# A two-layer graph network: the turn of z by a crossbar transpose DMA in place of TensorE, and two weight slots in place of three

## The reference

```
h = max(layernorm(x), 0);  x = x + GAT(relu(GAT(h, W1, ...)), W2, ...)    # layers 1 and 2
h = max(layernorm(x), 0);  x = x + GCN(relu(GCN(h, W1, ...)), W2, ...)    # layers 3 and 4
gat_conv: h = x @ W;  alpha = softmax over each node's edges of leaky_relu(a_src[src] + a_dst[dst]);  out = segment_sum(alpha * h[src]) + b
gcn_conv: h = x @ W;  out = segment_sum(h[src] * dinv[src] * dinv[dst]) + b
```

## Time and profile before

| | |
|---|---|
| three runs | 2389.22, 2389.45, 2395.45 us |
| median | 2389.45 us |
| span of the profiled execution | 2395.2 us |
| instructions | 45,199 |
| PE, PEld busy | 95%, 61% |
| DVE, ACT, POOL busy | 67%, 39%, 39% |
| DMA | 482.51 MB, mean 201 GB/s |

### The profile page before, as it was taken

The page is one execution under the profiler, slowest core; times in us unless marked ns, Lnnn a source line. Parts: engine busy times, 40 slices in busy tenths (PEclk is TensorE's granted clock), DMA queues, the critical chain, the costliest instruction groups (busy, mean ns, idle before and its releaser), DMA issues.

```text
span 2395.2 us, 45199 instructions
## 1 busy us (share of the span) xinstructions
PE 2277.9 (95%) x14017; PEld 1464.0 (61%) x14017; DVE 1607.5 (67%) x3699; ACT 940.8 (39%) x1271; POOL 933.2 (39%) x1469
## 2 busy tenths in 40 slices
PE   5999999999999999999999999999999999999954
PEld 3666666666666666666566666665666666666621
DVE  5788877775577675443699999655556666668732
ACT  2333343333344454334354445333333434333311
POOL 2333324431534442211366565455433333234354
PEclk9999999999999999999999999999999999999966
DMA  4333332225455554343688888776689988777666
GB/s 167 112 115 116 117 108 98 99 93 184 149 188 192 187 189 151 127 157 118 203 273 288 288 285 276 242 229 216 227 264 308 304 301 303 240 239 258 229 216 203
DMA packets 150732, 482.51 MB, mean 201 GB/s; under 512 B 22265, under 2 KB 22344, under 8 KB 150516
## 3 DMA queue, kind: packets, MB, share of 16 engines
q1 hardware_dynamic: 112804, 308.94, 36.7%
q0 software_dynamic: 37840, 172.47, 23.2%
HBM read 262.87 MB, written 225.76 MB: 204 GB/s over the span
## 4 chain that ended last, share of the span: by engine, by line
PE 68%; DVE 11%; issue 8%; DMA 8%; POOL 4%; ACT 1%; DVEq 0%; POOLq 0%; ACTq 0%
PE ps_h L870 56%; PE ps_z L857 7%; DMA row_in<-in_x,idx_b 4%; DVE bn L1046 2%; DVE pre L1042 2%; DMA edge_mem<-rows,idx_d 2%; DVE pre L1040 2%; PE ps_e L888 1%; DMA out<-base_out,idx_o 1%; PE ps_e L941 1%; PE ps_e L942 1%; DVE edge_mem L1104 1%; POOL rstd L566 1%; POOL edge_mem L551 1%; POOL idx_b L617 1%
## 5 line engine op out<-in xcount | busy, mean ns | idle before, releaser
L870 PE MATMUL ps_h<-w_hi,z_hi 128*128 128x384 f16 x3792 | 929.5, 327 | 0.0
L870 PE MATMUL ps_h<-w_lo,z_hi 128*128 128x384 f16 x3792 | 929.1, 327 | 0.0
L870 PE MATMUL ps_h<-w_hi,z_lo 128*128 128x384 f16 x3792 | 928.7, 327 | 0.0
L1079 DVE TENSOR_TENSOR z_lo<-ps_z,z_hi 128x768 f16<-128x768 f32 x316 | 301.8, 955 | 357.9 <-ACT z_hi L778 354.8
L870 PEld LDWEIGHTS ps_h<-w_lo,z_hi 128*128 128x128 f16 x3792 | 372.0, 98 | 247.2 <-issue 3.0
L870 PEld LDWEIGHTS ps_h<-w_hi,z_lo 128*128 128x128 f16 x3792 | 371.9, 98 | 246.9 <-issue 2.7
L870 PEld LDWEIGHTS ps_h<-w_hi,z_hi 128*128 128x128 f16 x3792 | 372.2, 98 | 219.2 <-issue 15.9
L771 ACT ACTIVATE row_out<-ps_h,grow 128x768 f32<-128x768 f32 x237 | 213.1, 899 | 544.0 <-PE ps_h L870 543.7
L857 PE MATMUL ps_z<-ident,z 128*128 128x128 f32 x1896 | 264.8, 277 | 42.4 <-ACT z L789 35.4
L778 ACT ACTIVATE z_hi<-ps_z 128x768 f16<-128x768 f32 x316 | 254.2, 804 | 46.7 <-PE ps_z L857 46.0
L857 PEld LDWEIGHTS ps_z<-ident,z 128*128 128x128 f32 x1896 | 226.5, 143 | 72.5 <-ACT z L789 40.0
(11 more groups left out here) (213 smaller groups left out, 2324.5 us busy)
## 6 DMA issues: line engine op xcount, KB each, us to landing
rows<-row_out SPq DMA_DIRECT2D x316, 384.0 KB, 3.1
row_in<-rows SPq DMA_DIRECT2D x118, 384.0 KB, 4.2
x_rows<-pre SPq DMA_DIRECT2D x79, 384.0 KB, 4.3
row_in<-x_rows SPq DMA_DIRECT2D x79, 384.0 KB, 4.0
row_in<-in_x SPq DMA_DIRECT2D x78, 384.0 KB, 3.1
rows<-e_out SPq DMA_DIRECT2D x60, 384.0 KB, 3.9
w_raw<-in_L_gnn_W SPq DMA_DIRECT2D x4, 2304.0 KB, 10.0
base_rows<-base_out SPq DMA_DIRECT2D x20, 384.5 KB, 4.3
```

Source lines behind the costliest of these rows:

```text
L870: last = nc.tensor.matmul(ps_h[s][:, a, 0:HALF], zp[s][:, c, :], wp[:, c, a * HALF:(a + 1) * HALF], start=(c == 0 and zp is z_hi and wp is ...
L1079: V.tensor_tensor(pair3(z_lo[t.slot]), psum_pair(ps_z), pair3(z_hi[t.slot]), ALU.subtract).then_inc(z_lo_ready, 1)
```

## The change

z is split into its fp16 halves before it is turned. ACT makes z twice from the same rows, once to fp16 into the left half of z_half (128 x 1536, fp16) and once to float32. DVE subtracts and writes the right half. SP then issues one DMA that transposes the 12 blocks of 128x128 from z_half (two slots) into z_turn (four slots), and TensorE's turns, ps_z and the z_hi eviction are gone. The halves are made and turned two tiles ahead of their products; z, the preparation and the loads each move one tile further ahead, and the prologue has five windows in place of four.

```diff
-    t = 0 if phase["before"] else -4
+    t = 0 if phase["before"] else -5
-        w_hi = [sb(f"w_hi{s}", [P, KC, D], F16) for s in range(3)]
-        w_lo = [sb(f"w_lo{s}", [P, KC, D], F16) for s in range(3)]
+        w_hi = [sb(f"w_hi{s}", [P, KC, D], F16) for s in range(2)]
+        w_lo = [sb(f"w_lo{s}", [P, KC, D], F16) for s in range(2)]
-        w_of = {1: 0, 2: 1, 3: 2, 4: 0}
+        w_of = {1: 0, 2: 1, 3: 0, 4: 1}
-        z_hi = [sb(f"z_hi{s}", [P, KC, P], F16) for s in range(2)]
-        z_lo = [sb(f"z_lo{s}", [P, KC, P], F16) for s in range(2)]
+        z_half = [sb(f"z_half{s}", [P, 2 * D], F16) for s in range(2)]
+        z_turn = [sb(f"z_turn{s}", [P, 2 * KC, P], F16) for s in range(4)]
...
+            def turn(t):                                          # SP
+                wait(sp, z_lo_ready, t.g + 1)
+                sp.sem_inc(sp_gate, 1)
+                sp.dma_start_transpose(z_turn[t.slot4][:, :, :], z_half[t.slot][:, :]).then_inc(z_turned[t.slot4], 16)
...
             def window1(t, side, i, r):                           # SP; window() alike
                 if t.exists(-1):
                     store(t.plus(-1))
-                if t.exists(4) and t.plus(4).phase["layer"] == 1:
-                    load_x(t.plus(4))
+                if t.exists(2):
+                    turn(t.plus(2))
+                if t.exists(5) and t.plus(5).phase["layer"] == 1:
+                    load_x(t.plus(5))
...
-                if t.exists(1):                                   # ACT
-                    b = t.plus(1)
-                    wait(act, z_turned, b.g + 1)
-                    wait(act, h_ready, b.g - 1)
-                    nc.scalar.activation(pair3(z_hi[b.slot]), psum_pair(ps_z), ACT.Copy).then_inc(z_hi_ready, 1)
-                if t.exists(2):
-                    b = t.plus(2)
+                if t.exists(3):
+                    b = t.plus(3)
                     layer = b.phase["layer"]
-                    wait(act, z_turned, b.g - 1)
+                    wait(act, z_lo_ready, b.g - 1)
+                    if isinstance(b.g, int) and b.g < 2:
+                        pass
+                    else:
+                        act.wait_ge(z_turned[(b.slot4 + 2) % 4], (b.count(b.phase["g0"] - 2, 4) + 1) * 16)
...
+                        nc.scalar.activation(z_half[b.slot][:, 0:D], frm[:, :], ACT.Relu, bias=nmr[b.slot4][:, 0:1],
+                                             scale=rstd[b.slot4][:, 0:1])
...
             def products(t, side_step):                           # PE
-                wait(pe, z_lo_ready, t.g + 1)
+                pe.wait_ge(z_turned[t.slot4], (t.slot4_uses + 1) * 16)
...
             def low_parts(t):                                     # DVE, now of t+2
-                wait(dve, z_hi_ready, t.g + 1)
-                V.tensor_tensor(pair3(z_lo[t.slot]), psum_pair(ps_z), pair3(z_hi[t.slot]), ALU.subtract).then_inc(z_lo_ready, 1)
+                wait(dve, z_ready, t.g + 1)
+                V.tensor_tensor(z_half[s][:, D:2 * D], z[s][:, :], z_half[s][:, 0:D], ALU.subtract).then_inc(z_lo_ready, 1)
```

More of the change, by code:

```diff
@@ L489, in window @@
             def window(t, side, i, r):
-                if t.exists(4) and t.plus(4).phase["name"] in ("3f", "4f"):
-                    load(t.plus(4))
+                if t.exists(5) and t.plus(5).phase["name"] in ("3f", "4f"):
+                    load(t.plus(5))
                 if t.exists(-1):
                     store(t.plus(-1))
+                if t.exists(2):
+                    turn(t.plus(2))
                 b = t.plus(1)
@@ L502, in window @@
                     sp.dma_start(row_in2[b.slot][:, :], x1_rows[bass.ds(b.pos * P, P), :]).then_inc(x1_loaded[b.slot], 16)
-                b = t.plus(3)
-                if t.exists(3) and b.phase["layer"] == 3:
+                b = t.plus(4)
+                if t.exists(4) and b.phase["layer"] == 3:
                     wait(sp, x1_ready, b.pos + 1)
@@ L573, in window1 @@
                     find_positions(i * 4 + r)
-                if t.exists(3) and t.plus(3).phase["layer"] == 1:
-                    norm_factors(t.plus(3))
-                if t.exists(4) and t.plus(4).phase["layer"] == 2:
-                    load(t.plus(4))
+                if t.exists(4) and t.plus(4).phase["layer"] == 1:
+                    norm_factors(t.plus(4))
+                if t.exists(5) and t.plus(5).phase["layer"] == 2:
+                    load(t.plus(5))
                 if side == "order+mask":
@@ L649, in window @@
             def window(t, side, i, r):
-                if t.exists(4) and t.plus(4).phase["name"] != "4f":
-                    load(t.plus(4))
+                if t.exists(5) and t.plus(5).phase["name"] != "4f":
+                    load(t.plus(5))
                 b = t.plus(-1)
@@ L792, in window @@
                         act.wait_ge(shrink_ready, top_count(b) + 1)
+                        nc.scalar.activation(z_half[b.slot][:, 0:D], pre[b.slot][:, :], ACT.Relu,
+                                             scale=shrink[b.slot4][:, 0:1])
                         nc.scalar.activation(z[b.slot][:, :], pre[b.slot][:, :], ACT.Relu,
@@ L852, in _ @@
         def _(pe):
-            def turn(t):
-                wait(pe, z_ready, t.g + 1)
-                wait(pe, z_lo_ready, t.g)
-                for c in range(KC):
-                    last = nc.tensor.transpose(ps_z[:, c // 3, (c % 3) * P:(c % 3 + 1) * P],
-                                               z[t.slot][:, c * P:(c + 1) * P], ident[:, :])
-                last.then_inc(z_turned, 1)
             def products(t, side_step):
                 layer, s = t.phase["layer"], t.slot
-                wait(pe, z_lo_ready, t.g + 1)
+                pe.wait_ge(z_turned[t.slot4], (t.slot4_uses + 1) * 16)
                 wait(pe, row_ready, t.g - 1)
@@ L867, in products @@
                 for c in range(KC):
-                    for zp, wp in ((z_hi, hi), (z_hi, lo), (z_lo, hi)):
+                    for half, wp in ((0, hi), (0, lo), (KC, hi)):
                         for a in range(2):
-                            last = nc.tensor.matmul(ps_h[s][:, a, 0:HALF], zp[s][:, c, :], wp[:, c, a * HALF:(a + 1) * HALF],
-                                                    start=(c == 0 and zp is z_hi and wp is hi),
-                                                    stop=(c == KC - 1 and zp is z_lo))
+                            last = nc.tensor.matmul(ps_h[s][:, a, 0:HALF], z_turn[t.slot4][:, half + c, :], wp[:, c, a * HALF:(a + 1) * HALF],
+                                                    start=(c == 0 and half == 0 and wp is hi),
+                                                    stop=(c == KC - 1 and half == KC))
                     if c == KC - 1:
@@ L892, in window @@
                 layer = t.phase["layer"]
-                if t.exists(1):
-                    turn(t.plus(1))
                 if t.i is None and t.at == 0 and layer > 1:
@@ L1275, in window @@
                     result(t.plus(-1))
-                if t.exists(1):
-                    low_parts(t.plus(1))
+                if t.exists(2):
+                    low_parts(t.plus(2))
                 if edges and r % 2 == 0:
```

54 lines of the change are left out of this document (28 added, 26 removed).

## The result

| | before | after |
|---|---|---|
| median of four runs each | 2391.28 us | 2553.59 us (2529.84 to 2563.07) |
| ratio, 95% interval | | 1.067 [1.061, 1.073] |
| span of the profiled execution | 2395.2 us | 2542.6 us |
| PE, DVE, ACT, POOL busy | 95, 67, 39, 39% | 85, 63, 39, 39% |

The change costs 6.7%. The forecast was 2233 us, its own range up to 2320; the wide range, up to 2750, holds the time, but the forecast was of a faster kernel.

The account below looks back on a forecast made before the run. TensorE was taken as the bound (PE busy 95%); removing its turns, limited by DVE and DMA in some stages, gained 161 us, less 3.9 at the start: 2389.45 - 157 = 2233 us. Own range 2185 to 2320, wide range 2185 to 2750.

Parts of the forecast that it names:

- price (c): How long one transpose DMA holds the 16 DMA engines: 1.0 us taken, 12.0 us as the other end.
- The sign that the prediction named for (c): DMA share in layer 1 would rise from 0.34 to 0.53; 0.9 would mean the transposes hold the DMA engines.
- rival R1: Transposes hold DMA engines T us each, slowing layers 3 and 4: 2650 us at T = 3.5, decides from 2.1; chance 0.20.
- If it may not, the rank stage loses its 25 us: Layer 1's rank stage: its 25.3 us gain needs DVE to be allowed to fall behind while its load waits behind the turn.
- the z_half ring: Two z_half slots: landing, two activations, z_lo and hand-overs, 10.5 us for two tiles, 5.3 a tile, under 5.85 of products.
- Price (a): SP's time to issue one transpose: 4.1 us taken, at a plain issue per block; ends 0.34 and 13.4 us.
- Price (b): Landing of one transpose after issue starts: 3.1 + 3.8 = 6.9 us.
- Layer 3's rest at 6.19 us: Layer 3's windows after its edge windows: 0.60 us gained in each of 36, 21.6 us together.
- z_lo at 955 ns: DVE's subtraction for the low half, now with fp16 output from SBUF, keeps its 955 ns; bounds 0.5 and 1.0 us.
- the second z on ACT at no cost: ACT's extra fp16 activation, at most 1027 ns, replaces an 804 ns eviction; 4.0 us of a window over 6, so 0.
- the full 0.66 us: TensorE's six transposes per tile, removed from 316 tiles: 207.6 us if TensorE stays the bound everywhere.
- R2: Blocks transposed one after another at a generated-row price hold SP's queue or the ring 13.4 us a tile: 4640 us; chance 0.12.

Follow-up runs that it names:

- the run with the load ahead: Changed kernel, in layer 1 SP issues the load of x for tile t+5 ahead of the turn of tile t+2: 2525.66 us, ratio 1.056.
- With the ring cut: Changed kernel without transpose DMA (zeros in z_turn), z_lo's source in PSUM, layer 3's norm factors one tile later from window 44 on: 2223.22 us, ratio 0.930.
- another queue: Changed kernel with the transposes issued by ACT in its own queue instead of by SP: 2880.55 us, ratio 1.204.
- Thin gathers: Changed kernel with the edge gathers' rows cut from 3 KB to 64 bytes, same count of rows: 2389.06 us, ratio 1.000.
- the mixed kernel: Changed kernel's schedule, DMA turning only 73 tiles where few gathers run, TensorE the others: 2370.23 us, ratio 0.993; 2362.45 with norm factors late from window 44.

## Why the prediction was wrong

The time splits into three measured steps, which the forecast had as one: turns at no cost, 2389 to 2267 (-122); their bytes as a plain copy, to 2333 (+66); the transpose in place of the copy, to 2554 (+221).

*The failed step is price (c)*, "I take 1.0, nearest to the stretches in which the engines are at their limit". It was taken from stretches of plain transfers, which it fits (0.94 us); the transpose holds the engines 2.57 us, between the ends 1.0 and 12.0 that stood there. The sign that the prediction named for (c), the DMA share in layer 1, says the same: 0.53 was forecast, 0.62 and 0.72 came, and 0.62 x 7.88 - 0.34 x 6.94 is 2.5 us a tile.

2.57 lies past the 2.1 from which rival R1 decides, and R1's outcome came, a slower kernel, but its mechanism explains only part. With 2.57 for T, its sum, share times window plus T, gives about 2457 us (an estimate from the earlier trace rows), some 97 too few. For layer 3's edge windows it gives 8.8 us (8.79 measured, but that is luck: 7.94 stand there without any transfer, and the same code took 9.43 in another run). It gives 6.6 for layer 2's edge windows (8.18), where the collapse beside the gathers is missing, and 8.9 for layer 4's (7.81), where the share passed 1.0 and was no limit. And R1 had layer 1 gain 47 us; it lost 31, by the ring of the rank stage. No row of the kernel before showed a transpose, so (c) should have been left open, with more than 0.20 on R1.

*"If it may not, the rank stage loses its 25 us"*: the condition was named and put aside. It may not: DVE has 5.72 us of work in a window and waits for the load that stands behind the turn. The stage lost 43 us instead of gaining 25. As the run with the load ahead showed, the queue's order is under a third of the 1.42 us over no turn. The wait that is left is that of the z_half ring, which was set at 5.3 us a tile without ACT's waits and SP's in it. A plain copy in the same place leaves the stage at 7.44, so most of this loss comes from waiting for a transfer at all, not from its being a transpose.

*Price (a)*, 4.1 us of SP: a median of 2.30, about 1.5 in layer 1, so it was too high as a rule and too low at its worst, beside gathers. A fixed issue time was the wrong model. *Price (b)*, 6.9 us: the median landing was 6.4, but up to 19.5.

*Layer 3's rest at 6.19 us* assumed that TensorE bounds it, from a window 0.3 us above TensorE's work. Free turns left it at 7.17. No row that the prediction rests on shows what the other engines wait for in that stage, so the ring was not seen. With the ring cut, free turns give 2223 us; the forecast of 2233 (its own sum makes 2232) needed both that cut and a transfer that costs nothing.

*Right*: z_lo at 955 ns (949 measured), the second z on ACT at no cost, and the full 0.66 us where nothing else binds (layer 4's rest without the turn, 6.48 to 5.84; layer 2's rest even 0.83). R2 did not come: it needed 13.4 us a tile in SP's queue or the ring, and the median issue is 2.30 us, the median landing 6.4. The Trainium skill, "VectorE: DVE Perf Modes", section "The three transpose paths", has 1309 ns for one 128x128 two-byte block by the crossbar, and twelve in series would be, as an estimate, 15.7 us; in this trace all twelve land after 6.4 us in the median, 3.6 at the least, so by that figure the blocks overlap. The Trainium skill, "DMA: Bandwidth & Descriptors", section "Latency and other measured facts", has 261 GB/s for a transposing DMA with a non-contiguous middle dimension, the lower of the two rates that the prediction weighed; as an estimate this would hold the engines 1.5 us. The 2.57 us here are 153 GB/s. The measurement decides: both rates are too good for the transposes of this kernel.

*Not isolated*: the two weight slots, the moved hooks and the number of z_half slots, which no run changed alone. Why a transpose collapses beside the edge gathers isn't settled either. The runs show that it takes both and that another queue doesn't help. Thin gathers end it in layer 2, but whether by their fewer bytes or by the smaller part of the table that they read, no run tells.

## What to carry to other kernels

Price a new kind of transfer by its smallest row and by what runs beside it, not by its bytes, and try the plain copy of the same bytes beside it: the difference of two short runs told here what no row of the kernel before could. A stage whose window is a few tenths above an engine's work may be held by a ring through several half-idle engines, and then a faster engine gives nothing there. Put such a change in by stages: the crossbar pays where the DMA engines have room (a share of 0.35 and 0.42 before) and no edge gathers run, and the mixed kernel kept only those windows.

## What the runs showed of the hardware

- The time of a transpose's issue depends on the traffic: 1.3 us at the least, up to 12.4 us beside edge gathers on SP's queue and 18.9 on ACT's. What stands behind it in that engine's order waits: 461.8 us in 104 waits of ACT.
- 269 transfers whose result only SP waits for cost 5.7% as transposes and 0.3% as plain copies.
- DMA shares of 1.24 to 1.39 stood beside 65 to 88 GB/s, and 1.01 beside 410: a full share says nothing of the bytes moved.
- A DVE subtraction with all operands in SBUF takes as long as one from PSUM (949 and 955 ns), but beside it a one-column operation on POOL takes 674 ns in the median in place of 188, and 186 again with the source in PSUM.
